# Layer 1 from a transposed, unscaled x: the first projection without degrees, the hop accumulators scaled in PSUM

## The reference

```python
norm = dis[row] * dis[col]        # dis = 1/sqrt(in-degree), 0 where there is none
def _tagconv(x, src, dst, norm, W, b):
    out = x @ W[0]
    h = x
    for k in range(1, K + 1):
        msg = norm[:, None] * h[src]
        h = jax.ops.segment_sum(msg, dst, num_segments=x.shape[0])
        out = out + h @ W[k]
    return out + b
h = relu(_tagconv(x, ..., W1, b1)); h = relu(_tagconv(h, ..., W2, b2))
return _layernorm(x + _tagconv(h, ..., W3, b3))
```

## Time and profile before

| | us |
|---|---|
| median of 3 runs | 1734.61 |
| lowest, highest | 1729.87, 1739.51 |
| the profiled execution: its time, and its span | 1746.28, 1744.5 |
| mean granted TensorE clock of it | 0.875 of full |
| PE, PEld, DVE, ACT, POOL busy | 1413.3, 650.8, 635.7, 358.3, 815.7 |

### The profile page before, as it was taken

The page is one execution under the profiler, slowest core; times in us unless marked ns, Lnnn a source line. Parts: engine busy times, 40 slices in busy tenths (PEclk is TensorE's granted clock), DMA queues, the critical chain, the costliest instruction groups (busy, mean ns, idle before and its releaser), DMA issues.

```text
span 1744.5 us, 19821 instructions
## 1 busy us (share of the span) xinstructions
PE 1413.3 (81%) x7597; PEld 650.8 (37%) x7597; DVE 635.7 (36%) x1623; ACT 358.3 (21%) x863; POOL 815.7 (47%) x909
## 2 busy tenths in 40 slices
PE   5888887878788897879787978889778977897777
PEld 4544443334233342324232433334233433342233
DVE  7854532323233353214221423334223322333334
ACT  6654431201011121102110111112001101111112
POOL 7544445463533325553555344542544554455432
PEclk9998988888788898889888988889888988898778
DMA  4322223332222222332333222222322322233322
GB/s 144 120 74 70 73 77 98 100 103 69 80 70 70 70 63 88 96 100 69 103 106 94 75 73 75 83 76 64 94 88 80 94 88 85 86 101 99 99 86 68
DMA packets 86045, 150.42 MB, mean 86 GB/s; under 512 B 18200, under 2 KB 59831, under 8 KB 85944
## 3 DMA queue, kind: packets, MB, share of 16 engines
q0 software_dynamic: 39184, 107.00, 21.5%
q1 hardware_dynamic: 46760, 42.08, 7.5%
HBM read 116.90 MB, written 32.10 MB: 85 GB/s over the span
## 4 chain that ended last, share of the span: by engine, by line
PE 73%; issue 16%; another core or an unknown queue 5%; DVE 5%; ACT 1%; POOL 0%; DMA 0%; DVEq 0%; POOLq 0%
PE pb L1158 53%; PE pb L1068 7%; PE pb L1070 4%; PE pb L1087 3%; PE pb L987 2%; PE pb L1163 1%; PE pb L1136 1%; DVE pb L1500 1%; PE pb L1108 1%; DVE V L1471 1%; DVE gT L1449 1%; ACT A L873 1%; ACT t L953 0%; DVE w L1505 0%
## 5 line engine op out<-in xcount | busy, mean ns | idle before, releaser
L1158 PE MATMUL pb<-V,A 128*128 128x512 f16 x4104 | 1058.1, 402 | 202.5 <-issue 197.5
L830 POOL DMA_INDIRECT GB<-vh,KS x810 | 776.6, 959 | 889.8 <-PE pb L1087 505.5
L1158 PEld LDWEIGHTS pb<-V,A 128*128 128x128 fp8e4 x4104 | 407.9, 101 | 750.6 <-issue 370.4
L1500 DVE SCALAR_TENSOR_TENSOR pb<-pb,cst,t 128x256 f32<-128x256 f32 (+1 forms) x225 | 110.0, 489 | 626.6 <-ACT t L953 528.5
L953 ACT ACTIVATE t<-pb,cst 128x256 f32<-128x256 f32 (+1 forms) x250 | 118.3, 473 | 804.7 <-remote 466.8
L1068 PE MATMUL pb<-Whl,gT 128*128 128x512 f16 x576 | 222.4, 409 | 30.4 <-issue 23.6
L1070 PE MATMUL pb<-Whl,gT 128*128 128x256 f16 x576 | 166.4, 289 | 27.5 <-issue 27.2
L1471 DVE SCALAR_TENSOR_TENSOR V<-V,pb 128x256 f16<-128x256 f16 (+1 forms) x225 | 94.1, 420 | 102.7 <-ACT V L927 90.2
L927 ACT ACTIVATE V<-pb 128x256 f16<-128x256 f32 (+1 forms) x225 | 85.7, 383 | 135.5 <-DVE pb L1500 123.4
L1068 PEld LDWEIGHTS pb<-Whl,gT 128*128 128x128 f16 x576 | 58.9, 102 | 121.2 <-issue 72.4
L1505 DVE SCALAR_TENSOR_TENSOR w<-bb,cst,t 128x256 f32<-128x256 f32 (+1 forms) x50 | 24.1, 482 | 216.0 <-ACT t L953 164.9
(11 more groups left out here) (194 smaller groups left out, 608.6 us busy)
## 6 DMA issues: line engine op xcount, KB each, us to landing
vh<-V SPq DMA_DIRECT2D x216, 128.0 KB
GB<-vh,KS POOLq DMA_INDIRECT x810
xr<-in_x SPq DMA_DIRECT2D x24, 128.0 KB
out<-g SPq DMA_DIRECT2D x24, 128.0 KB
xr<-in_W SPq DMA_DIRECT2D x16, 128.0 KB
V<-in_x SPq DMA_DIRECT2D x4, 384.0 KB, 6.0
V<-in_x SPq DMA_DIRECT2D x3, 512.0 KB, 5.1
V<-in_W SPq DMA_DIRECT2D x2, 512.0 KB, 4.3
```

The lines of the kernel that those rows point to most:

```text
L830: pool.indirect_dma_start(GB[:, slot, :], None, vh[vbuf[(L, k + 1)]][:, :], bass.IndirectOffsetOnAxis(ap=KS[:, p:p + 1], axis=0))\
L1158: mm = pe.matmul(acc[:, :], A8[:, a, t * P:(t + 1) * P], src[:, a, :], start=False, stop=(n == NT - 1), skip_group_check=True)
L1500: dve.scalar_tensor_tensor(hi, hi, cst[0:r, 1, t:t + 1], lt, ALU.mult, ALU.add).then_inc(S["s_d1"], 1)
```

## The change

The host passes x a second time, transposed (`xt`). SP loads it in six pieces; ACT writes its high half times SX = 64 to `gT` (`x_high`), DVE the rest (`x_low`). Layer 1 has no transpositions, and neither POOL's scaling nor the `gT` writes of each tile. W[3] is loaded apart and split with scale SW = 1024; the other six blocks of W1 come singly through `xr` and are split by `w_high` and `w_low`.

The first projection (`first_projection`) is six matmuls of 256 columns into one block of 256; tiles 0 to 3 share banks 6 and 2 in pairs and are projected ahead of the degrees, 4 and 5 right behind them. It is evicted in three steps: ACT scales into the high half of V (by `cst[:,5]`), POOL multiplies that by 64 into `t1` (`enlarged`), DVE takes it from the scaled bank and writes the low half.

In the three hops of layer 1 the projection of a tile is a separate item "S" (`started`), issued within the loop of the tile before; ACT then multiplies the whole bank by `cst[:,7]` in place (`scale_start`), and PE waits for that (`s_pm`) ahead of the tile's first hop matmul. 25 banks a hop are scaled so.

```diff
-MEANWHILE = (6, 8, 14)
-AHEAD = 4
+AHEAD = 9
+BEHIND_P = {6: (4, 5), 7: (6,)}
+BEHIND_V = {3: (0, 1), 5: (2, 3), 6: (4, 5), 7: (6,)}
+SPLITS = {("V", 0, 3, 8): 3, ("V", 0, 3, 11): 4, ("V", 0, 3, 14): 5}
+PAIRED = (6, 6, 2, 2)
+MID_D, MID_G, LEAD = 8, 14, 16
...
-XC = (0, 3, 6, 9, 13, 17, 21, 24, 25)
+XC = (0, 4, 8, 12, 17, 21, 25)
...
-    out = [("T", 0, 0), ("T", 0, 1)]
-    for t in range(NT):
-        if t + 2 < NT:
-            out.append(("T", 0, t + 2))
-        out.append(("P", 0, 3, t))
+    out = [("P", 0, 3, t) for t in range(NT)]
...
+                if L == 0:
+                    if i + 1 < len(DENSE):
+                        out.append(("S", 0, k, DENSE[i + 1]))
+                    elif k > 0:
+                        out.append(("S", 0, k - 1, DENSE[0]))
+                    out += [("S", 0, k, tile_of(st)) for st in range(at, steps.get(i, at)) if st % GV == 0]
                 out.append(("P", L, k, t))
...
+            def enlarged(t):
+
+                r = P if t < NT - 1 else HALF
+                pool.wait_ge(S["s_a2"], t + 1)
+                if t >= RB:
+                    pool.wait_ge(S["s_v"], t - RB + 1)
+                pool.tensor_scalar(t1[0:r, t % RB, :], V[0][0:r, t, 0:F], SC, 0.0, ALU.mult,
+                                   ALU.add).then_inc(S["s_hs64"], 1)
...
+            for t in range(6):
+                enlarged(t)
+            place_edges()
+            for t in range(6, 10):
+                enlarged(t)
+            pass_edges()
+            for t in range(10, NT):
+                enlarged(t)
...
+            def x_high(c):
...
+                high, xs = x_part(c, 0)
+                act.activation(high, xs, ACT.Copy, scale=SX).then_inc(S["s_xh"], 1)
...
+            def scale_start(k, t):
+
+                act.wait_ge(S["s_pj"], s_no[(0, k, t)] + 1)
+                acc = PB[pe_no[(0, k, t)]][:, 0:512 if t < NT - 1 else F]
+                act.activation(acc, acc, ACT.Copy, scale=cst[:, 7, t:t + 1]).then_inc(S["s_pm"], 1)
...
+            def first_projection(t):
...
+                for c in range(2):
+                    for half, part in ((0, slice(0, F)), (0, slice(F, 512)), (1, slice(0, F))):
+                        mm = pe.matmul(acc, gT[:, t, c, half, 0:r], Whl[:, 0, c, 3, part],
...
+            def started(k, t):
...
+                for c in range(2):
+                    pe.matmul(high, gT[:, t, c, 0, 0:r], Whl[:, 0, c, k, low], start=(c == 0), stop=False,
...
+                for c in range(2):
+                    mm = pe.matmul(acc[0:r, 0:F], gT[:, t, c, 1, 0:r], Whl[:, 0, c, k, 0:F], start=False, stop=False,
+                                   skip_group_check=True)
+                mm.then_inc(S["s_pj"], 1)
...
+            def x_low(c):
...
+                dve.scalar_tensor_tensor(low, xs, SX, high, ALU.mult, ALU.subtract).then_inc(S["s_xd"], 1)
...
+            dve.wait_ge(S["s_c0"], 1)
+            dve.scalar_tensor_tensor(cst[:, 5, :], dg[:, 7, :], 0.5 * SV / (SX * SW), cst[:, 0, :], ALU.mult,
+                                     ALU.mult).then_inc(S["s_c5"], 1)
+            dve.scalar_tensor_tensor(cst[:, 6, :], dg[:, 7, :], 0.5 * SV * SC / (SX * SW), cst[:, 0, :], ALU.mult,
+                                     ALU.mult).then_inc(S["s_c5"], 1)
...
             kept(0)
+            x_low(2)
             kept(1)
```

More of the change, by code:

```diff
@@ L433, in trailing @@
             waiting = []
+        out += starts
+        starts = []
         out.append(it)
@@ L677, in _ @@
                     keep(L, k, n)
+                    if (L, k) == (0, 2) and 1 <= n <= RB:
+                        fetch_w(NW1 + n - 1)
             for n in range(NT):
@@ L858, in _ @@
             act.activation(lnb[:, 1, 0:2], onesf[:, :], ACT.Sqrt)
+            x_high(2)
+            for u in range(2):
+                w_high(u, Whl[:, 0, u % 2, 2, 0:F], g[:, 2 + u % 2, :])
             act.wait_ge(S["s_dg"], 1)
@@ L1007, in _ @@
             mm.then_inc(S["s_gc"], 1)
+            def first_projection(t):
+                e = pe_no[(0, 3, t)]
+                if e in user and t >= len(PAIRED):
+                    emptied(p_of[user[e]])
+                if bank_of[e] > 4 and t >= len(PAIRED):
+                    pe.wait_ge(S["s_ev"], len(groups_of(0)))
+                if t == len(PAIRED):
+                    pe.wait_ge(S["s_cp5"], 2)
+                pe.wait_ge(S["s_xd"], next(c for c in range(len(XC)) if t < XC[c]))
+                acc = first_acc(t)
+                r = P if t < NT - 1 else HALF
+                for c in range(2):
+                    for half, part in ((0, slice(0, F)), (0, slice(F, 512)), (1, slice(0, F))):
+                        mm = pe.matmul(acc, gT[:, t, c, half, 0:r], Whl[:, 0, c, 3, part],
+                                       start=(c == 0 and half == 0 and part.start == 0),
+                                       stop=(c == 1 and half == 1), skip_group_check=True)
+                mm.then_inc(S["s_ps"], 1)
+            pe.wait_ge(S["s_wl"], 1)
+            for t in range(len(PAIRED)):
+                first_projection(t)
             pe.wait_ge(S["s_pl5"], 2)
@@ L1135, in work @@
                     for a in range(NT - 1):
+                        for other in within.get(a, ()):
+                            work(other)
                         pe.matmul(acc[0:HALF, 0:F], AT[:, a, TC:TC + HALF], src[:, a, 0:F], start=False, stop=False,
@@ L1188, in _ @@
                 elif k == 3 and it[1] > 0 and hop_over:
                     within.setdefault(LATER[sum(map(len, within.values()))], []).append(it)
-                elif it[0] == "P" and (k, t) == (2, 0):
+                elif it[0] == "S":
+                    place = MID_G if starts else LEAD if it[1:] == (0, 2, DENSE[1]) else MID_D
+                    starts.append(it)
+                    within.setdefault(place, []).append(it)
+                elif it[0] == "P" and (starts or (k, t) == (2, 0)):
@@ L1432, in _ @@
                     onehots(MARKS[was])
-                if was == ("P", 0, 3, NT - 2):
+                if was in SPLITS:
+                    x_low(SPLITS[was])
+                if was == ("V", 0, 3, 5):
+                    for u in range(2):
+                        w_low(u, Whl[:, 0, u % 2, 2, F:512], g[:, 2 + u % 2, :])
+                if was == ("V", 0, 3, NT - 3):
                     turned()
```

338 lines of the change are left out of this document (208 added, 130 removed).

## The result

The changed kernel took **1747.93 us** (median of 9 runs, 1743.22 to 1757.73), the kernel before 1737.63 (9 runs, 1729.87 to 1740.66): ratio **1.0053**, 95% interval 1.0031 to 1.0075. The forecast was 1725.2, 0.5% faster, with a range of 1713 to 1738, from a median of 1734.6 in the three runs then known; the sign was wrong. The profiled execution of the changed kernel took 1748.46 us, 0.5 above its median; that of the kernel before lay 9 us above its median, so the two traces differ by 2.2 us and not by 10.

The account below looks back on a forecast made before the run. Outside the opening stage, where PE, DVE and ACT are near their limit, only PE's work and its supply were taken to count. Opening stage -9.9 and hop (0, 2) +0.5 turn 1734.6 into 1725.2 us, range 1713 to 1738.

Parts of the forecast that it names:

- Opening stage, 9.9 us gained: From the first transpositions to hop (0, 2)'s second destination tile: ends at 55.6 instead of 65.53 us.
- Rival 3: Opening stage: POOL and DVE exclude each other, so their work stands in a row; gain 7.6 us, 1727.5; chance 9%.
- Hop (0, 2), +0.5 us: Scalings and weight operations add 20 us of ACT, mostly given back by PE's projection; cost 0.5 us, bounded by 0 and 20.
- rival 2: Hop (0, 2): ACT sets PE's pace and all 20 us show, 1744.7; chance 6% in full, 13% in part.
- Hops (0, 1) and (0, 0), 0 us: Other two hops of layer 1: scalings cost nothing, as ACT has little to do and PE has 3.5 us of other matmuls.
- the bound of 34 us: Other two hops of layer 1: upper bound, one scaling for each of 50 banks if waits came at the worst place.
- rival 4: Instruction supply: moving instructions shifts stretches of little work, about 10 us either way, 1715 or 1735; chance 12%.
- Layers 2 and 3, 0 us: The later layers: the change was taken to cost or gain nothing there.
- The sum: Whole kernel: -9.9 + 0.5 = -9.4 us, so 1734.6 becomes 1725.2; forecast's chance 40%.

Follow-up runs that it names:

- the two variants: Changed kernel with scaling left out in hops (0, 1) and (0, 0), or projecting two tiles ahead in hop (0, 1): 1738.40 and 1739.35 us.
- after_third: The changed kernel unedited, run again on a chip with stretches: 1747.24 us, ratio 1.0052 to the kernel before.
- the pair that was to tell: Kernel before and changed kernel, each with a 1x128 POOL memset ahead of every gather in all nine hops: 1358.83 and 1352.64 us.
- short_pause: Changed kernel projecting two tiles ahead in hop (0, 1), plus a 1x128 POOL memset ahead of gathers in all hops but the first: 1498.17 us, ratio 0.8380.
- two_ahead: Changed kernel projecting each dense tile two tiles ahead instead of one in hop (0, 1): ratio 0.9958 without stretches, 0.9998 with them.

## Why the prediction was wrong, step by step

*Opening stage, 9.9 us gained: the right mechanism, too large a term.* The stage ended at 59.1 (58.82 and the matmul) where 55.6 was forecast and 65.53 stood before: 6.4 us, and 6.7 at the first gather (58.78, 65.48). One-hots began at 26.96 (27.2 forecast). Tile 12 was projected at 41.52, not 39.7: POOL came to `enlarged` for tile 6 only after the placing of edges (its last step at 35.74 for 1.25), and DVE waited for it. Tiles 12 to 24 took 12.6 us and not 11.3, at the forecast pace of 0.87 with a few waits, and what comes behind 4.9 and not 4.6; with the 1.8 us of tile 12 that is the 3.5 us that are missing. Rival 3 (7.6 us) is nearer, and five rows are of its kind: `enlarged` took 0.40 to 0.42 us in 20 of its 25 times, and 0.81 to 1.49 in the five in which a DVE instruction with two inputs in SBUF was under way or began with it; one is the 1.34 at 40.30, beside a split of x on DVE (39.88 to 41.37). That is 3.3 us of POOL's time; what of it reached the end of the stage no run tells. The Trainium skill, "SBUF — State Buffer", "Who interferes with whom", says that such a VectorE instruction and a GpSimd instruction that reads SBUF contend. These five places agree with it.

*Hop (0, 2), +0.5 us: right in the first pair, too low on other chips.* It took 195.2 us against 198.3 there, and PE waited for `columns` for 7.3 us, not more than the 21.4 of the earlier trace rows (with "issue" ahead of the same matmuls 25.8 against 27.5), so rival 2 didn't occur. But on the chips with 1740, 1782 and 1790 us the hop was 4 to 17 us longer than in the kernel before, and on the last two about 7 in the mean, as much as the opening stage had gained. Without stretches it was 1 us shorter. Which step of the changed order costs this beside stretches isn't shown.

*Hops (0, 1) and (0, 0), 0 us: the step that failed.* The prediction set "16 hop matmuls or 3.5 us between the start and the tile that needs it" against ACT's busy time of 26 of 180 us, and of the bound of 34 us it said that "nothing in the rows is near that". 13 us came in hop (0, 1) in the first pair's traces; 9 of them are shown to be this dependence, by the two variants. What it left out is that ACT, idle for most of that hop, is at times not able to work: 66.3 us in six stands of up to 17.0, a row of the trace of before. For hop (0, 2) it had read such a row (26.8 us), for hop (0, 1) ACT's busy time alone. The earlier trace rows showed ACT at 0.00 in such a stretch, and the text used it for rival 4 alone, as a matter of chance. Slack of 3.5 us against stands of up to 17 was the sum to make: (17.0 - 3.5) at most for each of five bursts, 68 us, less what PE stands there anyway. In hop (0, 0) PE had two such waits, 7.9 us, and the hop was 7.2 and 5.5 us shorter; this gain is not explained.

*Layers 2 and 3, 0 us: right within the spread of traces* (1093.8 against 1099.9 and 1096.5; two variants with the same instructions there took 1100.9 and 1091.6).

*The sum.* -6.7 and +13 leave +6 before the other hops' spread; the first pair measured +10.3, after_third +7.7. Where ACT never stands, the same sum is the forecast's with the opening stage at its true size: -5.8 measured, ratio 0.9957. That this ratio lies beside the forecast's 0.9946 is luck: 5.8 us of a kernel of 1285 against 9.4 of 1735.

*What stays open.* Leaving the scaling out brought the ratio from 1.0052 to 1.0002, 9 of the 16 us to 0.996, where the chip without stretches has it. The other 7 are of the size that hop (0, 2) gives back in the traces, but no experiment removed that loss, as the pair that was to tell fell on a chip without stretches, and the first pair's traces don't have it. Nor is it shown what is kept from ACT and PE while POOL issues gathers, or why some chips have it and others not. The Trainium skill ("Runtime: NRT & Kernel Launch", "Instruction fetch mechanics") calls the cost of refilling an engine's instructions mostly hidden. Whether the stretches are such refills no run here shows. PE's idle time ahead of its 4104 hop matmuls is 0.0 us on one chip, 187.3 to 216.9 under "issue" in the four traces of unedited kernels on chips with stretches, and 0.0 again with gathers every 1.63 us; if it is refilling, it was hidden on the first and not on the others.

## What to carry to other kernels

An idle engine is not always a free one: ahead of giving it a step that another engine needs soon, look at its longest stand "for something the profile can't name", and give the step more lead than that; here one tile more of lead was worth 8 us of the whole time and cost nothing on either kind of chip. A version that beats both kernels depends on the chip: with stretches short_pause (0.838), without them the changed kernel or two_ahead (0.996), and the pause costs 5.6% there; two_ahead was behind neither kernel on either. And a kernel of one core should be timed on more than one chip before a half per cent is believed.
